# A three-layer hybrid network: preparation and position-bias scores in one block, column tiles in the guess, turned experts

## Time and profile before

| what | us |
|---|---|
| median of 3 runs (1770.0 to 1770.23) | 1770.22 |
| profiled execution, its own time | 1775.4 |
| its span | 1773.6 |
| busy: TensorE 87%, VectorE 50%, ACT 48%, POOL 18% | 1535.2, 886.6, 852.8, 317.3 |
| preparation of L0, first work to end | 7.5 to 84.4 |
| scores of L0 | 88.0 to 453.3 |
| guess | 1101.8 to 1179.3 |
| experts, to the last addition | 1681.7 to 1768.1 |

### The profile page before, as it was taken

How to read it: one execution, slowest core, us unless ns; L and a number is a source line. 1 busy time by engine, 2 the same in 40 slices (tenths; PEclk the granted TensorE clock), 3 DMA queues, 4 the chain that set the end, 5 groups by cost and what they waited for, 6 DMA issues and landing times. The chain is left out here.

```text
span 1773.6 us, 29966 instructions
## 1 busy us (share of the span) xinstructions
PE 1535.2 (87%) x12396; PEld 772.9 (44%) x12396; DVE 886.6 (50%) x1357; ACT 852.8 (48%) x1161; POOL 317.3 (18%) x135
## 2 busy tenths in 40 slices
PE   6689999999677978999999997999999999448598
PEld 4222222222333755566566565654444444126254
DVE  2468888888733535776777774010001000357242
ACT  3467777777343444677777764122222222231521
POOL 0466666665210001000000000000000000020000
PEclk9589999999898987999999998999999999779889
DMA  1000000000020004343444420000000000000000
GB/s 61 1 2 2 2 2 2 3 2 2 1 77 15 1 1 166 136 156 131 161 167 167 149 102 1 1 0 1 0 1 0 0 0 0 29 0 4 1 0 24
DMA packets 20658, 69.63 MB, mean 39 GB/s; under 512 B 688, under 2 KB 17072, under 8 KB 18096
## 3 DMA queue, kind: packets, MB, share of 16 engines
q1 hardware_dynamic: 20240, 66.73, 10.1%
q10 hardware_dynamic: 288, 1.05, 0.2%
HBM read 33.17 MB, written 34.60 MB: 38 GB/s over the span
## 5 line engine op out<-in xcount | busy, mean ns | idle before, releaser
L489 POOL TENSOR_TENSOR l_work<-l_a_scores,l_work 128x2048 f32<-128x2048 f32 x64 | 233.0, 3642 | 129.7 <-PE banks L607 115.8
L1777 PE MATMUL banks<-s_h,pack_l2f_l3f 128*128 128x512 f32 x512 | 221.0, 592 | 0.0
L1804 ACT ACTIVATE s_h<-banks,pack_l2f_l3f 128x512 f32<-128x512 f32 x128 | 88.0, 688 | 241.8 <-PE banks L1777 175.7
L547 DVE TENSOR_TENSOR l_work<-banks,sc_negc 128x1024 f32<-128x1024 f32 x128 | 156.3, 1221 | 49.7 <-PE banks L654 32.8
L607 PE MATMUL banks<-l_work,pack_l 32*32 32x512 f32 x4096 | 159.8, 607 | 23.4 <-ACT l_work L509 19.7
L509 ACT ACTIVATE l_work<-banks,pack_l 128x1024 f32<-128x1024 f32 x128 | 142.7, 1114 | 76.2 <-PE banks L607 75.4
L1370 PE MATMUL banks<-pack_l2a,r_e 128*128 128x128 f32 x1024 | 142.6, 282 | 26.3 <-ACT r_e L1422 26.3
L1422 ACT ACTIVATE r_e<-banks,r_max 128x1024 f32<-128x1024 f32 x128 | 142.5, 1113 | 44.9 <-DVE r_max L1463 44.8
L1457 DVE TENSOR_REDUCE r_raw<-banks 128x1 f32<-128x640 f32 (+1 forms) x128 | 109.5, 856 | 104.6 <-PE banks L1351 104.6
L1777 PEld LDWEIGHTS banks<-s_h,pack_l2f_l3f 128*128 128x128 f32 x512 | 97.3, 190 | 122.5 <-issue 122.5
L1351 PE MATMUL banks<-r_k,r_q 32*128 32x128 f32 (+3 forms) x832 | 147.9, 464 | 1.1 <-DVE r_v L1295 1.1
(11 more groups left out here) (380 smaller groups left out, 2142.8 us busy)
## 6 DMA issues: line engine op xcount, KB each, us to landing
distances<-r_rd SPq DMA_DIRECT2D x16, 2048.0 KB, 6.3
r_band<-distances SPq DMA_DIRECT2D x16, 1536.0 KB, 7.0
pack_l2f_l3f<-pack_dram_l2f SPq DMA_DIRECT2D x1, 2212.5 KB, 10.2
pack_l2f_l3f<-pack_dram_l3f SPq DMA_DIRECT2D x1, 1248.5 KB, 5.3
pack_l<-pack_dram_l SPq DMA_DIRECT2D x1, 1093.0 KB, 6.4
residual<-x ACTq DMA_DIRECT2D x2, 512.0 KB, 7.6
out<-residual SPq DMA_DIRECT2D x2, 512.0 KB, 3.1
pack_l2a<-pack_dram_l2a SPq DMA_DIRECT2D x1, 715.0 KB, 4.7
```

Source lines behind the costliest of these rows:

```text
L489: pool.tensor_tensor(image(H1R[:, c % 3]), bc(a, 2, 16), bc(b, 3, HW), ALU.add).then_inc(sem("added"), 1)
L547: dve.tensor_tensor(image(H2M[:, (2 * c + part) % 3]), image(PS[:, MAX + j:MAX + j + 2]), bc(NEGC[:, j:j + 2, n, i, rows(half)], 3, HW), A ...
L1777: ins = pe.matmul(bank, W["w2"][:, col:col + P], H1[:, c, m], start=(m == 0), stop=(m == HB - 1))
L1804: act.activation(H[:, c, k], PS[:, g % 8], ACT.Tanh, bias=bias).then_inc(sem("tanh"), 1)
```

## The change

Three parts change.
- `l0_bias` puts preparation and scores into one block of one stage, with one set of semaphores. POOL and VectorE wait in the scores for the evictions that they read (`written`), `offsets(1)` waits for the copies and masks, and the ring `H1R` starts one place further on. VectorE evicts A of units 0 to 10 and B of 0 to 13, ACT A of 11 to 15 and B of 14 and 15, all after its eight hats. `layer1` is spread over the samplings by `WITH_SAMPLE`.
- `l2_guess` writes the two halves of the second layer, and the lift of b2, to partitions 0 to 63 and 64 to 127 of one bank. One tanh takes both; the products to the nodes use rows 0 to 63 and 64 to 127; one copy is on VectorE and one on ACT.
- `l3_experts` has hidden units on the partitions and tokens in the columns. The selection is made in four column tiles and turned. The weights are turned back and spread over the 128 hidden units of four experts by products with 0 and 1 (`gates`), and VectorE multiplies them with the relus in `HT`. The values add up over the 8 rounds in four banks, and the four transfers of the output are in the same block.

The diff, cut to its core; lines that are only indented otherwise are left out, and of functions printed above most of the removed lines.

```diff
@@ -192,257 +192,294 @@
     return p
...
-def l0_prepare(nc, X, PS, W, loaded, KM, VT, Q, A, B, NF, SPARE, x_in):
+UNITS = NB * HEADS
+LOOPED = 12
+WITH_SAMPLE = (2, 1, 2, 1, 1, 1, 1, 1)
+A_ON_ACT = (11, 12, 13, 14, 15)
+B_ON_ACT = (14, 15)
+def unit(u):
+    return u % NB, u // NB
+def evicted(on_act, u, act):
+    return sum((k in on_act) == act for k in range(u + 1))
+def l0_bias(nc, X, PS, W, loaded, KM, VT, Q, A, WORK, NF, SALL, x_in):
     with ExitStack() as ctx:
         st = Stage(nc, ctx)
+        block = ctx.enter_context(nc.Block())
+        l0_prepare(st, block, X, PS, W, loaded, KM, VT, Q, A, WORK, NF, x_in)
+        l0_scores(st, block, PS, W, KM, Q, A, WORK, NF, SALL)
+def l0_prepare(st, block, X, PS, W, loaded, KM, VT, Q, A, WORK, NF, x_in):
     sb, sem = st.sb, st.sem
...
     s1 = sb("l0_s1", [P, 1])
...
-        UNITS = NB * HEADS
-        unit = lambda u: (u % NB, u // NB)
-        A_ON_ACT = (3, 7, 11, 13, 14, 15)
-        a_done = lambda u, act: sum((k in A_ON_ACT) == act for k in range(u + 1))
-        block = ctx.enter_context(nc.Block())
...
-            for u in range(UNITS - 2):
+        for u in range(LOOPED):
             if u not in A_ON_ACT:
...
-            b_out(UNITS - 2)
+        b_out(LOOPED)
         dve.wait_ge(sem("k"), 1)
...
-            b_out(UNITS - 1)
+        b_out(LOOPED + 1)
...
+        def b_out(u):
+            b, g = unit(u)
+            n = b * HEADS + g
+            act.wait_ge(sem("ab"), u + 1)
+            act.activation(B[:, :, n // 2, 2 * (n % 2):2 * (n % 2) + 2].rearrange("p r i x -> p i r x"),
+                           PS[:, 2 * b + 1].rearrange("p (i r x) -> p i r x", i=2, r=2), ACT.Copy
+                           ).then_inc(sem("b_act"), 1)
         for c in range(8):
             hat(c)
-                if c in (1, 3, 5):
-                    a_out(2 * c + 1)
-            a_out(13)
-            a_out(14)
+        for u in range(LOOPED - 1, UNITS):
+            a_out(u)
+            if u in B_ON_ACT:
+                b_out(u)
         for n in range(2):
...
-            a_out(15)
...
+        def free(u):
+            mine = u in A_ON_ACT
+            pe.wait_ge(sem("a_act" if mine else "a_dve"), evicted(A_ON_ACT, u, mine))
+            mine = u in B_ON_ACT
+            pe.wait_ge(sem("b_act" if mine else "b_dve"), evicted(B_ON_ACT, u, mine))
         def layer1(u):
...
-                    mine = u - 2 in A_ON_ACT
-                    pe.wait_ge(sem("a_act" if mine else "a_dve"), a_done(u - 2, mine))
-                    pe.wait_ge(sem("b_out"), u - 1)
+                free(u - 2)
             for c in range(2):
...
-                if c < 6:
-                    layer1(2 * c + 2)
-                    layer1(2 * c + 3)
+            at = 2 + sum(WITH_SAMPLE[:c])
+            for u in range(at, at + WITH_SAMPLE[c]):
+                layer1(u)
             sample(c)
+        layer1(12)
+        layer1(13)
         pe.wait_ge(sem("kv"), 1)
...
+        free(UNITS - 2)
+        free(UNITS - 1)
+        pe.wait_ge(sem("b_dve"), evicted(B_ON_ACT, UNITS - 1, False))
...
@@ -451,228 +488,237 @@
     eng.sem_inc(passed, 1)
...
-def l0_scores(nc, PS, W, KM, Q, A, WORK, NF, SALL):
-    with ExitStack() as ctx:
-        st = Stage(nc, ctx)
+def l0_scores(st, block, PS, W, KM, Q, A, WORK, NF, SALL):
     sb, sem = st.sb, st.sem
...
-        block = ctx.enter_context(nc.Block())
+    last_unit = lambda n: 4 * (n % PAIRS) + 2 + n // PAIRS
+    def written(eng, u, b_too):
+        for name, on_act, act in (("a_dve", A_ON_ACT, False), ("a_act", A_ON_ACT, True)):
+            if evicted(on_act, u, act):
+                eng.wait_ge(sem(name), evicted(on_act, u, act))
+        for name, on_act, act in (("b_dve", B_ON_ACT, False), ("b_act", B_ON_ACT, True)):
+            if b_too and evicted(on_act, u, act):
+                eng.wait_ge(sem(name), evicted(on_act, u, act))
...
+            if c % 8 == 0:
+                written(pool, last_unit(n), True)
+            if c == 2:
+                pool.wait_ge(sem("sampled"), 8)
             a = A[:, n, 8 * i:8 * i + 4]
             b = B[:, 0, n, i].rearrange("p (u y) -> p u y", y=HW)[:, :, rows(half)]
-                pool.tensor_tensor(image(H1R[:, c % 3]), bc(a, 2, 16), bc(b, 3, HW), ALU.add).then_inc(sem("added"), 1)
+            pool.tensor_tensor(image(H1R[:, (c + 1) % 3]), bc(a, 2, 16), bc(b, 3, HW), ALU.add).then_inc(sem("added"), 1)
...
+            if c % 8 == 0:
+                written(dve, last_unit(n), False)
             dve.wait_ge(sem("negb"), c // 4 + 1)
...
-            for b in range(NB):
-                offsets(b)
+        offsets(0)
+        pe.wait_ge(sem("vt_out"), 2)
+        pe.wait_ge(sem("vm"), NB)
+        pe.wait_ge(sem("km"), NB)
+        offsets(1)
         constants()
...
@@ -1591,13 +1637,14 @@
...
-    p.add("to_nodes", np.concatenate([nodes, row * np.ones((1, NB * NODES), np.float32)]))
+    p.add("to_nodes", np.tile(nodes, (2, 1)))
+    p.add("b2_lift", np.concatenate([np.zeros_like(nodes), row * np.ones((1, NB * NODES), np.float32)]))
     steps = np.tile(integration(NODES, np.arange(PIX) * DT), (NB, 1))
...
-    p.add("ident", np.eye(NB * NODES, dtype=np.float32))
+    p.add("ident", np.tile(np.eye(NB * NODES, dtype=np.float32), (2, 1)))
     return p
...
@@ -1610,7 +1657,7 @@
         YN = sb("g_y", [P, N])
...
-        H2 = sb("g_h2", [N, HB * P])
+        H2 = sb("g_h2", [P, HALF_H])
         G = sb("g_g", [P, HB, N])
...
@@ -1624,10 +1671,8 @@
                                      ).then_inc(sem("base"), 1)
...
-                for h in range(2):
-                    dve.wait_ge(sem("g"), 2 * g + h + 1)
-                    dve.tensor_copy(G[:, 2 * h:2 * h + 2].rearrange("p m n -> p (m n)"), PS[:, 3 + h, 0:2 * N]
-                                    ).then_inc(sem("g_out"), 1)
+                dve.wait_ge(sem("g"), g + 1)
+                dve.tensor_copy(G[:, 0:2].rearrange("p m n -> p (m n)"), PS[:, 3, 0:2 * N]).then_inc(sem("g_dve"), 1)
                 dve.wait_ge(sem("moved"), g + 1)
...
@@ -1644,10 +1689,11 @@
                     act.wait_ge(sem("z1"), g * HB + k + 1)
...
-                for h in range(2):
-                    act.wait_ge(sem("z2"), 2 * g + h + 1)
-                    act.activation(H2[:, h * HALF_H:(h + 1) * HALF_H], PS[0:N, 1 + h, 0:HALF_H], ACT.Tanh
-                                   ).then_inc(sem("h2"), 1)
+                act.wait_ge(sem("z2"), g + 1)
+                act.activation(H2[:], PS[:, 1, 0:HALF_H], ACT.Tanh).then_inc(sem("h2"), 1)
+                act.wait_ge(sem("g"), g + 1)
+                act.activation(G[:, 2:4].rearrange("p m n -> p (m n)"), PS[:, 4, 0:2 * N], ACT.Copy
+                               ).then_inc(sem("g_act"), 1)
             for n in range(1, NCH, 2):
...
@@ -1663,29 +1709,28 @@
                     pe.matmul(PS[:, FIRST[k], 0:N], W["w1"][:, k * P:(k + 1) * P], YN[:], start=True,
...
+                    pe.matmul(PS[N * h:N * h + N, 1, 0:HALF_H], W["b2_lift"][N:N + 32],
+                              W["to_steps"][N:N + 32, h * HALF_H:(h + 1) * HALF_H], start=True, stop=False,
+                              tile_position=(N, N * h), skip_group_check=True)
+                for m in range(HB):
+                    pe.wait_ge(sem("h1"), g * HB + m + 1)
                     for h in range(2):
...
                         c = m * HB * P + h * HALF_H
...
+                        ins = pe.matmul(PS[N * h:N * h + N, 1, 0:HALF_H], H1[:, m], W["w2"][:, c:c + HALF_H], start=False,
+                                        stop=(m == HB - 1), tile_position=(0, N * h), skip_group_check=True)
                 ins.then_inc(sem("z2"), 1)
                 last = g == GUESSES - 1
+                pe.wait_ge(sem("h2"), g + 1)
+                for j in range(2):
                     for h in range(2):
...
+                        half = slice(N * h, N * h + N)
+                        ins = pe.matmul(PS[:, 3 + h, j * N:j * N + N], H2[half, j * P:(j + 1) * P],
+                                        W["ident" if last else "to_nodes"][half], start=True, stop=True,
+                                        tile_position=(N * h, 0))
                 ins.then_inc(sem("g"), 1)
...
+                    pe.wait_ge(sem("g_act" if m // 2 else "g_dve"), g + 1)
                     w3 = W["w3"][:, m * P:(m + 1) * P]
...
@@ -2255,84 +2300,120 @@
     return p
...
+def l3_experts(nc, X, XN, PS, W, out_dram, stored):
     with ExitStack() as ctx:
...
+        GWT = sb("ex_w_t", [P, CH])
+        SPREAD = sb("ex_spread", [P, EXPERTS, EH])
+        HT = sb("ex_ht", [P, EB, NCH, CH])
+        AHEAD = 3
+        ACC, CHOICE, TURNED, GATES = 4, 4, 5, 6
+        quarter = lambda n: slice(32 * n, 32 * n + 32)
         block = ctx.enter_context(nc.Block())
...
+            def select():
+                for n in range(NCH):
+                    ins = pe.matmul(PS[quarter(n), CHOICE], W["select"], XN[:, n * CH:(n + 1) * CH], start=True, stop=True,
```

(90 more changed lines are left out.)

898 lines of the change are left out of this document (406 added, 492 removed).

## The result

The changed kernel takes 1740.14 us (median of four runs, 1739.63 to 1741.48), the kernel before 1770.22 on the same chip: ratio 0.9832, 95% interval 0.9814 to 0.9849, 30.1 us less. The prediction was 1737 with a range of 1728 to 1748. The profiled execution took 1739.63, its span is 1737.8. The execution profiled of the kernel before was 5.2 above its median, so the two traces differ by 35.8 us, not by 30.1. I therefore compare stage lengths, and where executions of one stage differ, several of them.

What follows compares the result with a forecast made beforehand. TensorE's own length was taken to bound experts and guess; no engine was full in L0's preparation. Guess -16, experts -13.4 and L0 -3.7 sum to -33.1 off the 1770.2 median: 1737 us, range 1728 to 1748.

Steps and rivals of the forecast that it cites:

- Guess: In `l2_guess`: lift and second layer in column tiles shorten each of eight guesses; -16 us, bounds -12 and -18.
- the walk: In `l2_guess`: step-by-step timing of one new guess, from first layer to next guess; 6.9 to 7.4 us, taken 6.95.
- the rival in which it falls: In the guess: TensorE's idling drops the clock, a guess takes 11.7 us at half clock; up to 1775 us, chance 0.03.
- rival 3: Guess and experts' selection: column tiles don't overlap, guess saves nothing, selection costs 6.8; 1737 + 16 + 3 = 1756 us, chance 0.04.
- Experts: In `l3_experts`: fewer selection products and turns, `gates` added, TensorE ends earlier; -13.4 us, bounds -9 and -16.
- The end of the span: Behind the experts' last addition: quarter transfers start when ready and the separate block goes; only 0.5 us taken.
- L0: Preparation and scores: new order starts offsets earlier, joined blocks move the semaphore clears; -3.7 us, bounds -9 and +1.
- -7.1: In L0's preparation: sampling 7 ends at 70, so offsets start at 80.9 instead of 88.0; -7.1 us.
- About 3.4 comes back: Behind L0's scores: the 39 semaphore clears moved there by the join are uncovered; about +3.4 us.
- rival 2: L0 gives nothing: preparation at TensorE's half-clock pace, clears in full at 453; 1742 us, chance 0.11.

## Why the prediction was right, and where it was off
**Guess: right.** Predicted 16 less, measured 16.6 in the stage and 15.6 alone. A guess takes 6.82 (predicted 6.9 to 7.4; the walk itself adds up to 6.84 and was rounded up). The tanh starts 1.99 after the second layer, as walked (1.71 and 0.28). Behind the first guess the clock stayed at 1.00, so the rival in which it falls did not happen in this kernel. TensorE waits 0.48 in a guess and not 0.7; the earlier trace rows, which I had set against that rival, show only 0.29 of idling in a window at 1.00 and were weak support. The kernels with dealt clears show what half clock costs here: 12.15 for a first guess, where I had 11.7 for each. The price of rival 3 was too low by 2 in my sum: a selection of 6.8 instead of 1.8 is 5 more, not 3. The rule of the Trainium skill that I had weighed ("TensorE: Matmul & The Clock Gate", Part 3, "The mechanism": a weight load overlaps with running products only where the row group differs) is not borne out by this trace: the two column tiles share their row groups, and the 16 records take 1.95 instead of 3.67, with 1.49 us of weight loads inside them.

**Experts: right in sum.** Predicted 13.4 less, measured 14.2 in the trace and 14.5 alone. `gates` costs 1.07 (1.15), later rounds 8.13 and 4.70 (7.9 and 4.6), and no wait stands after the second round. Two terms were off against each other, and the match is in part luck. The clock rose at 1664, 4 us into the stage, where I had it rise after 5 to 10, and `gates(0)` started 15.1 us after the stage's start instead of 17.1. Then it fell again in the first round, which cost 2.0 (in two other executions it did not). The end of the span came 1.75 sooner behind the last addition, where I had taken 0.5: that term was too small by 1.2.

**L0: mechanism right, size wrong.** The step is the "-7.1" in -7.1 + 3.4 = -3.7. A weight costs 3.02 and not 2.8, since one unit of `layer1` alone takes 2.01 and not 1.75, nearly as long as two; with two units in two of the rounds sampling 7 is over at 73.55, not at 70 and outside the 66 to 72.3 that I had allowed, and the offsets start at 83.73, not 80.9. Against other executions of the kernel before, whose scores began between 83.9 and 88.3, the start is some 4 us earlier and not 7. "About 3.4 comes back" was somewhat high: 2.77, with 0.8 more in the next gap and in the attention. What is left is within 1 us. The forecast of 1737 took in 3.7 for this part; the range held the result all the same. What happened is rival 2, "L0 gives nothing", to which I gave 0.11. My reading that no engine was full in the preparation was true of the old order; the new order fills TensorE, at half clock, and its length is then the bound.

**Sum.** 16.6 + 14.2 + about 0.8 is 31.6 by the traces, 30.1 by the medians; 33.1 was predicted. Most of the 3 us between is the L0 term, 3.7 predicted and about 0.8 left.

What stays open: what makes the clock hold or rise in the preparation. In the new order TensorE has no idle time, and in six executions without the added product the clock is 0.50 from 48 to 72; in the two with it, it is at 1.00 from 60 on. In the old order it rises without the product too, from 56 in one execution and from 64 in another, and lies between 0.50 and 0.79 in the other three. So the clock rose in every execution with the full-array product, but the product is not the only thing that can bring the rise, and a narrower or a row-tiled one of the same length was not tried. Nor was the new order tried with its units in pairs, which by the 2.01 and 2.09 above should shorten TensorE's work there without any added product.

## What to carry to other kernels
Ask of a stage that is to be packed closer which engine will be full afterwards, and at what clock: in L0 the new order filled TensorE with small tiles at half clock and won nothing that the runs can tell, while one full-array product in each round, work that nobody needs, won 2.5 us by the end of the scores and 4 to 6 by the ratios. Keep tiles together that overlap: a unit issued alone took 2.01, two together 2.09. Joining two blocks only moves the clearing of their semaphores; to make it cheaper, deal it to several engines (7 us here), and look at the clock in the stages behind. Look at more than one execution before a fall or a rise of the clock is put down to an edit. Splitting a narrow product into two column tiles of one bank nearly halves it (3.67 to 1.95), and turning the weights of the experts (8 turns) instead of their hidden values (128) took whole rows off the chain.

## What the runs showed of the hardware that I had not expected
- TensorE busy 4.00 of 4 over 28 us with the granted clock at 0.50 (records 32*128 and 128*32, the changed kernel). With a 128*128 product of 256 columns before each sampling the clock was at 1.00 from 60 to 76 us. The Trainium skill ("TensorE: Matmul & The Clock Gate", Part 1) says that the clock is set by how busy TensorE has recently been; if busy is what the trace counts as busy, this case does not agree.
- Two waits of TensorE of 0.8 us, with 1.2 us of work between them, were followed by a fall of the clock to 0.71 in the next window of the changed kernel, and in five of seven executions in all; in the other two, with the same waits, it held 1.00.
- Clearing 38 more semaphores on one engine cost 2.77 us, 0.07 each. Dealt to four engines the same gap fell from 4.66 to 1.77, and the eight products behind it took 1.07 instead of 1.94. But in all three kernels with dealt clears the guess took 5 us longer, with the clock at 0.50 through the first guess and most of the second.
- A product pair in two of four row groups (x4, one unit) took 2.08 at half clock, two such pairs in all four row groups (x8) 2.09; at full clock 1.13 and 1.14.
- A product with `start` set, written to columns 256 to 511 of bank 7, changed sums that were under way in columns 0 to 127 of that bank; without `start` it did not. The Trainium skill says as much ("PSUM — Partial Sum Buffer", The four PSUM rules: it clears the marks of the whole bank by which later products are added, so that the next product of a sum under way overwrites it), and this run agrees.
